# A transformer pair on one core: the opening is folded into one block with the recurrent stage, which begins when two chunks are normalised

## What is computed

```python
mod = (silu(L0_c) @ L0_wmod).reshape(4, 6, 1, 256)
sa, ca, ga, sb, cb, gb = (mod[:, n] for n in range(6))
ga = (2 * (ga >= 0) - 1) * maximum(abs(ga), 0.25)          # gb alike
h = layernorm(x) * (1 + ca) + sa                            # x: 4 x 512 x 256
x = x + ga * recurrent_attention(h)
h = layernorm(x) * (1 + cb) + sb
x = x + gb * hadamard_ffn(h)
...                                                         # layer 1, with its own mod

# recurrent_attention: q, k, v = silu(h @ W_qkv), q and k normalised;
# lr0, lr1, lr2 = softplus(h @ W_lr + b_lr + const), per token and head
def step(w0, w1, w2, chunk):                                # 8 chunks of 64 tokens
    gate, hb = k @ w0, k @ w2
    hidden, dhidden = silu(gate) * hb, v @ w1.T
    g1 = newtonschulz5((hidden * lr1).T @ v)
    g0 = newtonschulz5((k * lr0).T @ silu_backprop(dhidden * hb, gate))
    g2 = newtonschulz5((k * lr2).T @ (dhidden * silu(gate)))
    w0, w1, w2 = each w + g, its columns brought back to their first norms
    return silu(q @ w0) * (q @ w2) @ w1
```

## Time and profile before

| | us |
|---|---|
| median of 3 runs | 1109.02 |
| lowest and highest | 1106.84, 1109.79 |
| profiled execution | 1106.67 |
| its span in the trace | 1104.9 |
| gates of step 0, of step 1, of step 2 | 81.10, 118.52, 157.77 |

### The profile page before, as it was taken

One profiled execution on the slowest core, in us unless ns is written; L12 is line 12 of the kernel. 1 busy time (PEld: TensorE's weight loads), 2 busy tenths in 40 slices (PEclk: granted clock), 3 DMA queues, 4 the chain that ended last, 5 costly groups with the idle time before them and its releaser, 6 DMA issues.

```text
span 1104.9 us, 26014 instructions
## 1 busy us (share of the span) xinstructions
PE 1045.2 (95%) x10262; PEld 756.2 (68%) x10262; DVE 696.2 (63%) x2084; ACT 553.2 (50%) x1428; POOL 434.7 (39%) x391
## 2 busy tenths in 40 slices
PE   5988999999999999999999899999999999999978
PEld 2747788878887855574648667675867576757646
DVE  5219889889889952213232776756675676667774
ACT  2438777887787742212132453535454445444531
POOL 1022203303514711101003574756567565778720
PEclk8589999999999999999999899999999999999999
DMA  9300000000000002800003000300030002100202
GB/s 338 129 1 1 2 1 0 0 0 0 0 1 2 2 1 49 281 1 1 1 0 77 20 20 21 77 20 20 21 77 21 20 21 57 41 20 21 77 3 78
DMA packets 24207, 42.19 MB, mean 38 GB/s; under 512 B 6576, under 2 KB 14768, under 8 KB 22704
## 3 DMA queue, kind: packets, MB, share of 16 engines
q1 hardware_dynamic: 24112, 40.87, 12.4%
HBM read 21.98 MB, written 2.10 MB: 22 GB/s over the span
## 4 chain that ended last, share of the span: by engine, by line
PE 51%; DVE 5%; ACT 2%; issue 1%; POOL 0%; DVEq 0%
PE quad L1948 9%; PE quad L1597 7%; PE quad L1990 7%; PE quad L2010 7%; PE quad L1993 5%; PE quad L1892 5%; PE quad L2024 5%; PE quad L2088 1%; PE quad L1956 1%; ACT act_probs L2246 1%; DVE act_probs L2346 1%; PE quad L1483 1%; ACT act_probs L2255 1%; PE quad L1911 1%; DVE wq_wo L2360 1%
## 5 line engine op out<-in xcount | busy, mean ns | idle before, releaser
L2599 POOL TENSOR_TENSOR act_probs<-act_probs,rden 128x512 f32<-128x512 f32 (+3 forms) x128 | 171.0, 1339 | 155.9 <-DVE rden L2365 155.8
L2246 ACT ACTIVATE act_probs<-act_probs,neg_max 128x256 f32<-128x256 f32 (+3 forms) x256 | 140.8, 552 | 82.6 <-DVE neg_max L2346 82.3
L1948 PEld LDWEIGHTS quad<-hT,ug_queries 128*128 128x128 f32 x1024 | 120.5, 194 | 30.6 <-issue 18.6
L1948 PE MATMUL quad<-hT,ug_queries 128*128 128x128 f32 x1024 | 132.2, 283 | 3.0 <-ACT act_probs L2255 2.2
L2346 DVE CUSTOM_DVE_ANT_0 act_probs<-quad,mask 128x256 f32<-128x256 f32 (+3 forms) x256 | 114.9, 486 | 6.4 <-PE quad L1993 6.0
L1597 PE MATMUL quad<-hT,ug_raw_switch 128*128 128x512 f32 x256 | 115.6, 602 | 0.0
L1990 PE MATMUL quad<-ckvT,ug_raw_switch 64*128 64x512 f32 (+3 forms) x512 | 105.6, 480 | 6.9 <-DVE neg_max L2346 6.9
L2365 DVE RECIPROCAL rden<-den 128x2 f32<-128x2 f32 x128 | 20.6, 161 | 121.1 <-ACT act_probs L2246 120.9
L1612 DVE SCALAR_TENSOR_TENSOR act_probs<-quad,ws_up,silu_keys 128x512 f32<-128x512 f32 x32 | 24.0, 751 | 102.4 <-ACT silu_keys L1607 102.4
L1597 PEld LDWEIGHTS quad<-hT,ug_raw_switch 128*128 128x128 f32 x256 | 48.1, 193 | 55.5 <-issue 54.7
L1607 ACT ACTIVATE silu_keys<-quad,ws_gate 128x512 f32<-128x512 f32 x32 | 22.0, 687 | 120.5 <-PE quad L1597 120.5
(11 more groups left out here) (318 smaller groups left out, 2361.8 us busy)
## 6 DMA issues: line engine op xcount, KB each, us to landing
rope_swapped<-gate SPq DMA_DIRECT2D x120, 64.0 KB, 2.0
wmod<-in_wmod SPq DMA_DIRECT2D x2, 1536.0 KB, 9.9
x_pairs<-in_x SPq DMA_DIRECT2D x2, 1024.0 KB, 9.8
x_rows<-x_pairs SPq DMA_DIRECT2D x8, 256.0 KB, 4.8
wq_wo<-in_wq_nopeT SPq DMA_DIRECT2D x1, 2048.0 KB, 8.6
wq_wo<-in_wo SPq DMA_DIRECT2D x1, 2048.0 KB, 12.9
down_raw_out<-x_pairs SPq DMA_DIRECT2D x16, 128.0 KB, 2.3
ug_queries<-in_switch_w SPq DMA_DIRECT2D x1, 2048.0 KB, 7.8
```

The lines of the kernel that those rows point to most:

```text
L1948: mm = nc.tensor.matmul(out[:, P * i:P * i + P], w[:, kt, HP * half + i, :], k.hT[:, kt, b, cols], start=(kt == 0), stop=(kt == KT - 1))
L2246: nc.scalar.activation(tile, tile, ACT.Exp, bias=neg_max[:, r, e:e + 1], scale=-1.0, accum_out=den[:, r, e:e + 1])\
L2599: nc.gpsimd.tensor_tensor(tile, tile, rden[:, t % RING, :].unsqueeze(2).to_broadcast([P, 2, cols]), ALU.mult)\
```

## The change

The two blocks become one, and its programs are written in this order:

- Loads: a third of layer 0's modulation weights, x in four transfers of two chunks each (the first two ahead of the rest), the identity, w_qkv, the learning rates' weights, the rest of x, state and weights; then the other five thirds of modulation weights, which land in tiles that the feed-forward weights use later, so that these are loaded only once the modulation products are made.
- Modulation is made as columns at once: the weights are the stationary side, 128x128, and the four columns of `silu_c` move (`make`, 8 products for the first two vectors, 16 for the rest of layer 0 ahead of step 0, 24 for layer 1 in the free place of `G_ORDER` in step 0). The gates are guarded as columns, transposed to rows of eight partitions in step 0, and `spread` copies them to all partitions by 16 transfers from SBUF to SBUF. GpSimd waits for these ahead of step 2.
- Normalisation goes by groups of two chunks. Groups 0 and 1 are done before step 0, a part of group 0 is shifted and scaled by VectorE; groups 2 and 3 are transposed in step 0 at places called `START`, into bank 6, and shifted and scaled by ScalarE between its copies.
- Learning rates: for chunks 0 and 1 before step 0; for the others by two passes with 32 padded columns for each of three groups (`project_rest`), a transpose and a second softplus, in and behind step 0. The softplus costs an exponential and a logarithm, each with a table load on ScalarE.
- Chunks 0 and 1 are projected from `hT`, without a copy. Chunk 0's q and k are scaled by VectorE; of chunk 1 one projection is made before step 0, the others behind its gates.
- The first norms, the scaling of w_proj and of the feed-forward signs move into and behind step 0.

```diff
+class Modulations:
...
+        homes = [(k.wq_switch, 0), (k.wq_switch, w), (k.wq_switch, 2 * w)], [(k.wq_switch, 3 * w), (k.w_vo, 0), (k.w_vo, w)]
...
+    def make(self, pe, l, parts):
+        for part in parts:
+            n, half = divmod(part, 2)
+            for m in range(KT):
+                at, lo = self.column(l, part, m), D * half + P * m
+                for kt in range(KT):
+                    mm = self.k.nc.tensor.matmul(self.bank[:, at:at + B], self.w[l][n][:, kt, lo:lo + P], self.silu[l][:, kt, :],
+                                                 start=(kt == 0), stop=(kt == KT - 1))
...
+    def make_first(self, pe):
+        pe.wait_ge(self.silu_done, 2)
+        pe.wait_ge(self.first_in, 16)
+        self.make(pe, 0, (SHIFT_A, SCALE_A)).then_inc(self.made, 1)
+
+    def make_rest(self, pe):
+        pe.wait_ge(self.rest_in[0], 16 * 2)
+        pe.wait_ge(self.taken, 2)
+        self.make(pe, 0, (GATE_A, SHIFT_B, SCALE_B, GATE_B))
+
+    def make_next(self, pe):
+        pe.wait_ge(self.rest_in[1], 16 * 3)
+        self.make(pe, 1, (SHIFT_A, SCALE_A, GATE_A, SHIFT_B, SCALE_B, GATE_B)).then_inc(self.made, 1)
...
+    def spread(self, sp):
+        k = self.k
+        sp.wait_ge(self.rows_taken, 1)
+        for b in range(B):
+            i, j = divmod(b, 2)
+            sp.dma_start(k.gate_pairs[C * j:C * j + C, i, :], self.repeated(b, 0, C)).then_inc(self.gates_in, 16)
+            sp.dma_start(k.gates[0][:, b, :], self.repeated(b, D, P)).then_inc(self.gates_in, 16)
+        for b in range(B):
+            sp.dma_start(k.gates[1][:, b, :], self.repeated(B + b, 0, P)).then_inc(self.gates_in, 16)
+            sp.dma_start(k.gates[2][:, b, :], self.repeated(B + b, D, P)).then_inc(self.gates_in, 16)
...
+    def modulate_first(self, dve, src):
+        dve.wait_ge(self.turned, 2)
+        for b in range(B):
+            to, view, scale, shift = self.views(0, 1, b, src)
+            op = self.k.nc.vector.tensor_scalar(to, view, scale, shift, ALU.mult, ALU.add)
+        op.then_inc(self.first_half, 1)
...
-    INNER = ((A, 0), (A, 1), (OUT_ROWS, 1), (A, 2), (A, 3), (AA, 0), (A, 4), (AA, 1), (A, 5), (TURN_V, 0), (AA, 2), (OUT_ROWS, 0), (AA, 3), (Y, 0), (AA, 4), (AA, 5), (TURN_QK, 0), (Y, 1),
...
+    INNER = ((A, 0), (A, 1), (OUT_ROWS, 1), (START, 0), (A, 2), (A, 3), (AA, 0), (A, 4), (AA, 1), (START, 1), (A, 5), (TURN_V, 0), (AA, 2), (OUT_ROWS, 0), (START, 2), (AA, 3), (Y, 0), (AA, 4), (AA, 5), (START, 3), (TURN_QK, 0), (Y, 1),
...
+                if first:
+                    pe.wait_ge(first_norm.taken, 3)
+                    pe.wait_ge(w_in, STATE_IN)
+                else:
                     for q in (0, 1, 3, 4):
...
+                    project_qk(1, 1)
+                    project_v(1)
...
+                    elif first:
+                        mods.make_next(pe)
...
+                    elif ph == START and first:
+                        if n == 1:
+                            pe.wait_ge(mods.rows_taken, 1)
+                        elif 2 <= n < 6:
+                            pe.wait_ge(first_norm.taken, 2 + n)
+                        if n == 0:
+                            mods.make_rows(pe)
+                        elif n < 5:
+                            first_norm.turn(pe, 2 + (n - 1) // 2, (n - 1) % 2, bank[6])
+                        elif n == 5:
+                            rates.project_rest(pe)
+                        else:
+                            rates.turn_rest(pe)
...
+            pe.wait_ge(k.consts_set, N_CONSTS)
+            mods.make_first(pe)
+            pe.wait_ge(k.eye_in, 16)
+            for g in range(2):
+                for kt in range(KT):
+                    first_norm.turn(pe, g, kt, bank[NORM_PLACES[g][kt]])
+            pe.wait_ge(qkv_in, 16)
+            first_norm.wait_chunks(pe, 0)
+            project_qk(0, 0)
+            project_qk(0, 1)
+            rates.project_first(pe)
             project_v(0)
-            for i in range(PAIRS):
-                project_qk(i)
+            pe.wait_ge(s["qkv_acted"], 1)
+            project_qk(1, 0)
             pe.wait_ge(s["qkv_acted"], 3)
-            project_v(1)
-            for i in range(PAIRS):
-                project_qk(i)
             turn_v(0, 0)
-            turn_qk(0, 0, 4)
...
+            mods.take_silu(act)
+            act.wait_ge(k.consts_set, N_CONSTS)
+            act.wait_ge(mods.taken, 2)
+            first_norm.modulate(act, 0, 0, bank[NORM_PLACES[0][0]])
+            for kt in range(KT):
+                first_norm.modulate(act, 1, kt, bank[NORM_PLACES[1][kt]])
...
-            root_qk(0)
+            rates.exponential(act, 0)
             take_v(0, 0)
-            take_qk(0, 0, 4)
-            take_qk(0, 1, 6)
+            rates.logarithm(act, 0)
+            take_qk(0, 0, 1)
+            take_qk(0, 1, 3)
+            load_table(ACT.Silu)
...
+                if first:
+                    dve.wait_ge(s["qkv_acted"], 4)
+                    square_qk(1, 0, (0, 1, 2, 3))
+                    start_sums()
...
+                    if first:
+                        mods.take_rest(dve)
...
+            dve.wait_ge(k.eye_in, 16)
+            nc.vector.tensor_copy(k.eye_bf[:], k.eye[:])
+            mods.take_first(dve)
+            first_norm.sums(dve, 0)
+            first_norm.sums(dve, 1)
+            first_norm.normalize(dve, 0)
+            first_norm.normalize(dve, 1)
+            dve.wait_ge(mods.taken, 2)
+            first_norm.modulate_first(dve, bank[NORM_PLACES[0][1]])
+            first_norm.sums(dve, 2)
             for i in range(PAIRS):
                 dve.wait_ge(s["qkv_acted"], i + 1)
                 square_qk(0, i, (0, 1, 2, 3))
+            rates.start(dve, 0)
+            first_norm.normalize(dve, 2)
             norm_qk(0)
+            dve.wait_ge(s["qk_step"], 2)
+            dve.wait_ge(s["qkv_acted"], 3)
+            scale_first(0)
+            rates.one_more(dve, 0)
+            scale_first(1)
+            first_norm.sums(dve, 3)
+            rates.finish(dve, 0)
...
+            rates.finish(dve, 1)
+            dve.wait_ge(proj_in, 32)
+            nc.vector.tensor_scalar(w_proj[:], w_proj[:], onorm[:], None, ALU.mult)
+            ffn.scale_signs(dve)
...
+            pool.wait_ge(mods.gates_in, 16 * 4 * B)
...
+        def sync_program(sp):
+            mods.load_c(sp)
+            mods.load_w(sp, 0, 0)
+            for g in range(2):
+                sp.dma_start(k.x[:, 2 * g:2 * g + 2], I["x"][:, 2 * g:2 * g + 2]).then_inc(k.x_in[g], 16)
+            sp.dma_start(k.eye[:], I["eye"]).then_inc(k.eye_in, 16)
+            sp.dma_start(w_qkv[:], I["w_qkv"]).then_inc(qkv_in, 16)
+            rates.load(sp)
+            for g in range(2, 4):
+                sp.dma_start(k.x[:, 2 * g:2 * g + 2], I["x"][:, 2 * g:2 * g + 2]).then_inc(k.x_in[g], 16)
+            for i in range(PAIRS):
+                for j in range(2):
+                    sp.dma_start(state[:, 3 * j:3 * j + 3, H * i:H * i + H, :], I["state0"]).then_inc(w_in, 16)
+                    sp.dma_start(weight[:, 3 * j:3 * j + 3, H * i:H * i + H, :], I["weight0"]).then_inc(w_in, 16)
+            for l, n in ((0, 1), (0, 2), (1, 0), (1, 1), (1, 2)):
+                mods.load_w(sp, l, n)
+            sp.dma_start(w_proj[:], I["w_proj"]).then_inc(proj_in, 16)
+            sp.dma_start(onorm[:], I["onorm"]).then_inc(proj_in, 16)
+            for dst, name in ((k.had, "hadamard"), (k.su_ug, "su_ug"), (k.su_dp, "su_dp"), (k.ws_up, "ws_up"), (k.ws_gate, "ws_gate"), (k.ws_dp, "ws_dp")):
+                sp.dma_start(dst[:], I[name]).then_inc(k.ffn_in, 16)
+            sp.wait_ge(mods.made, 2)
+            raw = k.wq_switch[:].rearrange("p (w k n) -> p w k n", w=2, k=KT)
+            for dst, name in ((raw[:, 0], "w_upT"), (raw[:, 1], "w_gateT"), (k.w_vo[:].rearrange("p (m d) -> p m d", m=MT), "w_downT")):
+                sp.dma_start(dst, I[name]).then_inc(k.ffn_in, 16)
+            sp.wait_ge(first_norm.turned, 8)
+            mods.spread(sp)
+
```

636 lines of the change are left out of this document (291 added, 345 removed).

## The result

The changed kernel takes 1100.48 us (median of 19 runs, 1090.16 to 1103.69), the kernel before in the same comparison 1108.28 (1106.03 to 1111.78): ratio 0.9916, 95% interval 0.9896 to 0.9936. It is faster by 7.8 us, where 27.5 were forecast; 1094 was the upper end of the range.

What follows compares the result with a forecast made beforehand. Steps are bound by TensorE, and all before step 0's gates is opening. Terms -45.5 + 8.9 + 4.7 + 1.5 + 1.0 + 1.9 = -27.5 us on 1106.67 gave 1079.2, forecast 1081.5 as median; range 1072 to 1094.

Steps and rivals of the forecast that it cites:

- The opening: Everything before step 0's gates: they would start at 35.6 us instead of 81.10, a gain of 45.5 us.
- 2.1 of low clock: Projections of chunk 0 before step 0: 2.1 us added for a clock low at first; it might rise already at 19.
- The single-row transfers: Sixteen gate-spreading transfers: 10 us over 16 engines, 67 by one port; chance 0.03 for full loss, 0.03 for small delay.
- The 24 products between the column sums: Step 0, layer 1's modulation products after the first column sum: 5.1 us on the path, priced at full clock.
- 0.50 anywhere in step 0: Sign that the forecast is wrong: the granted clock is 0.50 anywhere in step 0.
- rival (B) in its first form: Clock stays low, step 0 at 1.2 GHz up to its middle: +9 us, 1090; chance 0.13 for (B).
- The middle: Middle of step 0: +4.7 us for ScalarE's excess work, +1.5 for the exponential's table load before the state updates.
- the 10 us: Sign that the forecast is wrong: step 0's middle grows by less than 4 or more than 10 us.
- The end and step 1: End of step 0: +1.0 us for ScalarE's table loads; step 1: +1.9 for VectorE's late rates and scalings.
- the forecast's 41.15 for step 1: Step 1 from gates to gates: 41.15 us, where it took 39.25 before.
- The further drain with each switch: ScalarE table switches: a skill's rule of about 1.4 us each, some 8 us more, about 1089; left out of the sum.
- the first part: Step 0 from gates to first scaled product: 20.4 us where it was 11.55, +8.9.

Runs made afterwards that it cites:

- e1_dram: Changed kernel with gate rows first written to DRAM and spread from there by 7 transfers instead of 16 single-row ones: 1085.20 us, ratio 0.9774 to the kernel before.
- e9_later: Changed kernel with twelve of the sixteen single-row transfers held back; they ran in steps 4 and 5: 1089.13 us, ratio 0.9828 to the kernel before.
- e5_row16: Kernel before plus twelve useless transfers of one SBUF row to 112 rows, from the start of step 0: 1113.30 us, ratio 1.0043.
- e6_row16_loop: Kernel before plus the same twelve useless transfers as e5_row16, issued in the loop from step 2 on: 1107.26 us, ratio 0.9996.
- e2_late: e1_dram with 16 of layer 1's 24 modulation products moved from behind the first column sum to the end of step 0: 1078.49 us, ratio 0.9726.
- e8_gfree: e2_late with layer 0's remaining modulation products moved into TensorE's first wait, and layer 1's last 8 moved before step 0's gates: 1079.65 us, ratio 0.9710.
- e13_early: e2_late with VectorE's side work (start-weight sums, last group's normalisation, w_proj and sign scaling) moved before step 0's backward part: 1079.46 us, ratio 0.9730.
- e3_row: Kernel before plus twelve useless transfers of one SBUF row to 127 rows, from step 2 on: 1108.20 us, ratio 0.9994.

## Why the prediction was wrong, point by point

**The opening (-45.5; measured -47.8).** Right. The chain is the one that was walked, and the 2.3 us beyond it are about the 2.1 of low clock that did not come: TensorE was at full rate from the first projections. The forecast had called both outcomes possible here, so this part of the gain is luck.

**The single-row transfers: the step that failed.** The prediction had found the place. It took the 27 GB/s of one port as "the edge, not a loss" and thought of one way only in which a long transfer can cost time: someone waits for it. The transfers did last 66 us, nobody waited for them, and step 1 lost 16.4 us against the forecast in three stops and the low clock behind them. e1_dram and e9_later give 16.4 and 18.3 us of step 1 back, from two sides, and e5_row16 makes a stop of the same kind in the kernel before. That the stops are code arriving late over the same engines fits every run: a piece in each of the four, TensorE going on 2.3 to 2.5 us behind it, and no stop where the same transfers met hardly any code. The Trainium skill (SBUF — State Buffer, Door 1: The DMA port swizzle) gives 27.2 GB/s for one port, an estimated 67 us; the trace agrees, 28 GB/s and 66 us. What was missing is on another page, the Trainium skill (Runtime: NRT & Kernel Launch, Instruction fetch mechanics): an engine's code is streamed in blocks of 16 KiB over a DMA queue of its own, and crossing a block is "mostly hidden". The pieces of 16 KB are in this trace. Of nine that arrived among single-row transfers (in the changed kernel, e5_row16, e6_row16_loop and e9_later) five were hidden; at the other four, with the engines 67 to 82% busy, TensorE stood for 2.7 to 6.0 us.

**The 24 products between the column sums (5.1; measured 8.3, and +3.3 in all).** The mechanism was right, VectorE's wait of 8.1 us with the column sums as releaser included. The price was taken at full clock, and the forecast's own sign for a mistake, 0.50 anywhere in step 0, came true: rival (B) in its first form, though smaller than its +9.

**The middle (+6.2; measured +11.4).** Mis-sized, and beyond the 10 us that the forecast had named as a sign of being wrong. The sum charged ScalarE's excess over its free room (4.7) and one table load (1.5). It treated the room in the middle as something that an engine can use at any time. The runs show a chain through one bank and three engines in program order, to which each part adds nearly its full length: at like clock 3.0 us for the 3.6 of ScalarE's modulations, 4.2 for the learning rates, and 4.3 are left with neither, the low clock at its start included.

**The end and step 1 (+1.0 and +1.9, together 2.9).** Together a little under, and the split differs from kernel to kernel: +0.45 and +1.88 in e1_dram, +2.07 and 0.01 in e9_later, +2.15 and 0.00 in e2_late. Where a low clock lengthens the end of step 0 (0.53 in the changed kernel, 0.61 in e9_later at 91 to 94.6 us, 0.74 in e2_late from 84 us on), VectorE's late work is done meanwhile and step 1 pays nothing. That e1_dram met the forecast's 41.15 for step 1 is luck in the split. The operations behind the three new table loads of step 0 began 1.29, 1.29 and 1.30 us after the load's start, and ahead of each load ScalarE stood for no more than 0.02 us. The further drain with each switch that the prediction quotes from the Trainium skill (ScalarE: Activation LUTs, What ACT_TABLE_LOAD costs), some 8 us by its count, is borne out nowhere here either.

**Sum.** With the stops removed (e1_dram) the gates of step 2 come 22.6 us earlier than before, against 27.5 forecast; the missing 4.9 are the 3.0 of the first part and the 4.3 of the middle, less 2.4 of better opening and end. With the stops, in the changed kernel, those gates come another 18.5 us later (17.8 later than in e9_later), and the median of the whole is 15.3 us higher. By its median e1_dram is 23.7 us faster than the kernel before, and its 1085.20 lie within the range of 1072 to 1094: what put the result outside it is the transfers. The forecast had given 0.06 to everything about them.

**What stays open.** Why the clock falls at 47 us in step 0, where it did not in the kernel before, is not settled: neither the few-column products (e2_late, e8_gfree) nor VectorE's order (e13_early) decides it. That a late piece of code is TensorE's own is argued from where it stops and from the like distance of 2.3 to 2.5 us between piece and going on; the trace names no engine for a piece. Why five of nine pieces cost nothing is open. The changed kernel's runs scatter over 13.5 us and those of e1_dram over 4.3; that a piece of code is not equally late each time would explain it and was not tested.

## What to carry to other kernels

Ask of a transfer not only who waits for it but how long it keeps the DMA engines busy and whether code is still arriving then: the share beside the GB/s tells it (0.8 at 28 GB/s), and idle TensorE with no releaser (in three of the four stops inside a group of equal products) is its mark. Spread rows from DRAM, not from one SBUF row, or do it in a loop that has run once. And where several engines hand a tile round through one bank, price each added operation at nearly its full length; here free room on each engine was no cover.

## What the runs showed of the hardware

- One SBUF row as the source of 128-row transfers: 27 to 29 GB/s over all sixteen engines, each packet holding its engine for about 0.4 us (0.779 x 16 engines x 67 us over 2035 packets). From DRAM each 512 KB transfer landed in a median of 5.9 us.
- 127 rows instead of 128: 24 GB/s, from one row or from all, and 3.0% of the sixteen engines' time, as if one engine had carried it all. The Trainium skill (DMA: Bandwidth & Descriptors, Why a DMA increments its semaphore by 16 and not by 1) says that a transfer of 127 partitions goes to one engine, and the 3.0% of e3_row agrees.
- Sixteen engines at 67 to 82% of such transfers, and a piece of code arriving: TensorE stopped for 3.18, 2.71, 6.04 (changed kernel) and 4.29 us (e5_row16), and went on 2.3 to 2.5 us after the piece.
- A stop is paid twice: behind the stops of 3.2, 2.7 and 6.0 us TensorE was granted 0.58, 0.66 and 0.51 for some 5 us each, though it was busy without a break.
